# Handing the maximum tiles to the groups of an attention unit by work instead of by count

## The reference, cut to what matters

```python
# 8 sequences of 1024 tokens, width 512, 16 heads of 32
Q, K, V = x @ W_Q.T, x @ W_K.T, x @ W_V.T        # split into 16 heads
attn = einsum('bhqd,bhkd->bhqk', Q, K) * 32 ** -0.5
attn = where(causal, attn, -inf)
y = softmax(attn) @ V
x = layernorm(x + y @ W_O.T)
x = layernorm(x + top1_expert_ffn(x))            # 8 experts, softmax router
```

## Time and profile before

| | |
|---|---|
| time, median of 3 runs | 2583.17 us (2582.08 to 2583.94) |
| profiled execution, its own time | 2585.2 us |
| its span | 2583.5 us |
| PE busy | 2358.2 us, 91% |
| DVE busy | 1452.3 us, 56% |
| ACT busy | 1021.9 us, 40% |
| POOL busy | 870.5 us, 34% |
| mean granted TensorE clock | 0.975 of full speed |

### The profile page before, as it was taken

One profiled execution on the slowest core, in us unless ns is written; L12 is line 12 of the kernel. 1 busy time (PEld: TensorE's weight loads), 2 busy tenths in 40 slices (PEclk: granted clock), 3 DMA queues, 4 the chain that ended last, 5 costly groups with the idle time before them and its releaser, 6 DMA issues. The chain is left out here.

```text
span 2583.5 us, 42271 instructions
## 1 busy us (share of the span) xinstructions
PE 2358.2 (91%) x14336; PEld 1529.8 (59%) x14337; DVE 1452.3 (56%) x3931; ACT 1021.9 (40%) x2089; POOL 870.5 (34%) x1531
## 2 busy tenths in 40 slices
PE   2999999999999999999999999999999999709998
PEld 1754675557554765476546755575547654508886
DVE  2666456735664466536664567355744665346665
ACT  2245414551445234622454245514452345133333
POOL 2223232333223332333232323332233222235665
PEclk9999999999999999999999999999999999859999
DMA  8532153314431353225321533144313421164444
GB/s 298 163 76 82 57 169 85 108 58 123 131 99 66 98 146 85 91 68 170 76 82 57 164 92 105 59 130 124 99 68 106 123 67 42 42 211 133 147 150 120
DMA packets 130937, 282.10 MB, mean 109 GB/s; under 512 B 33026, under 2 KB 42242, under 8 KB 128452
## 3 DMA queue, kind: packets, MB, share of 16 engines
q1 hardware_dynamic: 100920, 208.62, 27.3%
q0 software_dynamic: 28304, 70.64, 9.1%
q10 hardware_dynamic: 1536, 0.53, 0.1%
HBM read 133.04 MB, written 47.53 MB: 70 GB/s over the span
## 5 line engine op out<-in xcount | busy, mean ns | idle before, releaser
L675 ACT ACTIVATE probs<-score 128x512 f32<-128x512 f32 (+3 forms) x1216 | 563.0, 494 | 534.7 <-PE score L991 518.9
L924 PE MATMUL proj<-xt,w_qk 128*128 128x512 f32 x1536 | 428.7, 401 | 60.5 <-DMA w_qk<-w_qk_parts 58.4
L551 POOL TENSOR_SCALAR_AFFINE_SELECT probs<-probs 128x256 f32<-128x256 f32 x512 | 215.6, 423 | 785.3 <-ACT probs L675 782.4
L733 DVE CUSTOM_DVE_ANT_0 maxp<-maxp,mask_qk 128x384 f32<-128x384 f32 (+3 forms) x696 | 323.1, 507 | 233.4 <-PE maxp L979 231.8
L991 PE MATMUL score<-q_stack,k_stack 97*128 97x512 f32 (+2 forms) x1216 | 426.0, 373 | 22.2 <-ACT probs L675 19.8
L979 PE MATMUL maxp<-k_stack,q_stack 96*128 96x512 f32 (+2 forms) x1024 | 330.4, 366 | 35.4 <-DVE tile_max L728 16.3
L924 PEld LDWEIGHTS proj<-xt,w_qk 128*128 128x128 f32 x1536 | 285.6, 191 | 124.0 <-DMA w_qk<-w_qk_parts 49.6
L1011 PE MATMUL y_ps<-probs,v 128*32 128x512 f32 (+3 forms) x3072 | 329.4, 500 | 12.4 <-DVE rows L758 12.2
L1011 PE MATMUL den_ps<-probs,ones_f 128*32 128x512 f32 (+3 forms) x3072 | 320.9, 488 | 0.0
L991 PEld LDWEIGHTS score<-q_stack,k_stack 97*128 97x128 f32 x1216 | 224.6, 189 | 139.2 <-ACT probs L675 90.9
L979 PEld LDWEIGHTS maxp<-k_stack,q_stack 96*128 96x128 f32 x1024 | 181.4, 189 | 165.8 <-DVE tile_max L733 68.2
(11 more groups left out here) (144 smaller groups left out, 2864.7 us busy)
## 6 DMA issues: line engine op xcount, KB each, us to landing
w_qk<-w_qk_parts SPq DMA_DIRECT2D x64, 512.0 KB, 3.8
q_stack<-w_vo_parts SPq DMA_DIRECT2D x16, 2048.0 KB, 8.1
q_stack<-parts SPq DMA_DIRECT2D x512, 64.0 KB, 2.2
k_stack<-parts SPq DMA_DIRECT2D x512, 64.0 KB, 2.2
got<-dispatched SPq DMA_DIRECT2D x75, 257.0 KB, 2.5
xt_raw<-x_t SPq DMA_DIRECT2D x32, 512.0 KB, 4.3
q_stack<-parts POOLq DMA_DIRECT2D x256, 64.0 KB, 2.3
k_stack<-parts POOLq DMA_DIRECT2D x256, 64.0 KB, 2.5
```

The lines of the kernel that those rows point to most:

```text
L551: nc.gpsimd.affine_select(out=block, in_=block, compare_op=ALU.is_ge, fill=0.0, base=0, pattern=[[0, 2], [1, P]], channel_multiplier=-1)\
L675: nc.scalar.activation(probs[:, 4 * (n % PROBS) + h, c:BANK], score_bank(u, 4 * j + h)[:, c:BANK], ACT.Exp, scale=SCALE).then_inc(exp_done ...
L733: top = nc.vector.tensor_tensor_reduce(out=tile, in0=tile, in1=mask_qk[:, BANK - cols:BANK], scale=1.0, scalar=-3.0e38, op0=ALU.add, op1=A ...
L924: mm = nc.tensor.matmul(proj[bank][:, :], w_qk[:, o, ws, k, :], xt[:, xs, k, t * BANK:(t + 1) * BANK], start=c == 0, stop=c == 3 * KT - 1)
```

## The change

The tiles of a unit are no longer dealt out evenly by number over the groups. Each tile gets a work figure (4 for an unmasked tile, and for a diagonal one the sum over its heads of 1 + 3 * columns // 512, which is 4 or 3), each group a room: 2 for groups 6 and 7, and in units 1 and 2 also for groups 2 and 3, else 4. Tiles go in their order to the groups in proportion to room. In unit 0 the tiles now begin at group 1 instead of 2. Both engines read the same function `maxima`, PE at L1078 and DVE at L819.

```diff
-        MAX_GROUPS = (2, 10), (0, 9)
+        MAX_GROUPS = (1, 10), (0, 9)
 ...
             begin, end = MAX_GROUPS[u > 0]
             if not begin <= j < end or u + 1 == UNITS:
                 return []
-            return list(range(MTILES * (j - begin) // (end - begin), MTILES * (j + 1 - begin) // (end - begin)))
+            room = [2 if g in (HALF0 + LAG, HALF0 + LAG + 1) or u and g in (LAG, LAG + 1) else 4 for g in range(end)]
+            work = [4 if diag is None else sum(1 + 3 * cols // BANK for _ in heads) for _, heads, _, cols, diag in MAX_TILES]
+            upto = lambda g: sum(room[begin:g]) * sum(work) / sum(room[begin:end])
+            return [i for i in range(MTILES) if upto(j) <= sum(work[:i]) + work[i] / 2 < upto(j + 1)]
```

## The result

The changed kernel takes 2669.2 us (median of 4 runs, 2666.7 to 2673.6) against 2583.6 us (2582.1 to 2588.1) for the kernel before: ratio 1.033 [1.031, 1.035]. I had predicted 2622 us (2602 to 2639). The sign and the main mechanism were right; the size was less than half of it: +39 us predicted, +85.6 measured. The profiled execution's span is 2665.3 us, 81.8 more than before, and its mean granted clock 0.959 against 0.975. As shares of the span at half clock (twice what is missing from 1) that is about 219 us against 130.

The account below looks back on a forecast made before the run. The prediction took PE's ordered stream as the bound, busy 2358.2 of 2583.5 us. Its terms, -13.6 - 3.3 + 33 + 16.4 + 6.5 = +39 us on a median of 2583.2, gave 2622 us, range 2602 to 2639.

Parts of the forecast that it names:

- Unit 1, group 3, the main term: Unit 1, group 3: DVE takes tile 15 before `divide` and `low`, so PE stands 2.94 us a batch, 23.5 us in all.
- The copies: DVE's copies come later for PE's weighings: +0.7 and +0.5 us a batch in unit 1, +0.45 and +0.55 in unit 2.
- Unit 1's order and distribution: Unit 1: the stand in group 3 and the later copies together, +4.1 us a batch, +33 us.
- Unit 2: Unit 2: later copies and a wait at tile 19, +2.05 us a batch, +16.4 us, bounds 0.5 and 3 a batch.
- at tile 19, +1.05: Unit 2: tile 19 needs tile 16, which waits on DVE behind tile 15 and `divide`: +1.05 us a batch.
- Clock again: Unit 1: the 2.94-us stand loses the clock in four of eight batches, 1.6 us each: +6.5 us.
- Rival 3: Clock falls behind each stand of a batch, also those of 1.4 us in unit 2: 2635 us, chance 0.15.
- The term of unit 0: Unit 0: fewer waits of PE, -1.7 us a batch, -13.6 us, and clock no longer lost, -3.3 us.
- The stalls at tiles 19 and 28: Unit 0: PE's waits of 0.55 us in group 6 and 1.43 us in group 8 were to go.
- less waiting for ACT in group 1: Unit 0, group 1: ten matmuls fill PE's wait for ACT, 0.8 us a batch, of which 0.6 is given back.
- Rival 4: No gain in unit 0: bank waits in group 1 and the copy of group 6 take it; 2636 us, chance 0.10.
- the spacing of DVE's operations: On DVE the next operation starts 0.65 us after a 0.73-us masked reduction; whole lengths would add 3 us in all.

Follow-up runs that it names:

- experiment 1: Changed kernel, but in group 3 of units 1 to 3 DVE takes tile 15 behind the division and the `low`; ratio 1.009 to the kernel before.
- experiment 5: Kernel before, old distribution, but in group 3 of units 1 to 3 DVE takes all four tiles, 15 included, ahead of `divide` and `low`; ratio 1.022.
- experiment 3: Changed kernel, with the first matmul of tile 16 repeated 12 times in unit 1 and 7 times in unit 2; ratio 1.0231 to the kernel before.
- experiment 4: Changed kernel, with POOL's subtraction in unit 2's group 4 held until that group's exps are done; ratio 1.0266 to the kernel before.
- experiment 2: Kernel before, with the new distribution of tiles in unit 0 alone, units 1 and 2 keeping the old one; ratio 0.997 to the kernel before.
- experiment 8: Changed kernel with tile 15 behind division and `low`, and the last two tiles ahead of each copy reduced after copy and transposition; ratio 0.9944 to the kernel before.
- experiment 9: Kernel before, with three tiles ahead of the `low` in unit 0's groups 5 and 7, and one tile held back behind each copy; ratio 0.9906, 2556.6 us.
- experiment 7: Kernel before, but in groups 5 and 7 of unit 0 DVE takes three tiles before the `low`, not two; ratio 0.9966 to the kernel before.
- experiment 6: Changed kernel, with the `low` moved ahead of `divide` in group 3 of units 1 to 3; ratio 1.0244 to the kernel before.

## Why the prediction was right in sign and too small in size

**Right.** *Unit 1, group 3, the main term.* 2.73 us against 2.94, each link of the chain within 0.2 us, and experiments 1 and 5 give and take it. *The copies.* The two in unit 1 rose from 0.26 to 0.96 and by 0.5 us, as reckoned (+0.7, +0.5). Unit 1's order and distribution made 4.6 us a batch for 4.1 predicted. Unit 2's made 2.37 for 2.05, which is partly luck: at tile 19, +1.05 was reckoned, and in the last batch PE waits 0.44 us there; the copies came to +0.65 and, by experiment 1, +0.43 for 0.45 and 0.55 reckoned, and some 0.8 us had no term in the sum.

**The step that failed first: "Clock again", +6.5 us.** It took four losses of 1.6 us, all in unit 1. Measured were thirteen: six in unit 1 (12.8 us, since the stretch was 6.8 us long in three batches) and seven in unit 2 (17.3 us). The rule of the Trainium skill that stood beside that step ("TensorE: Matmul & The Clock Gate", What's actually happening: half clock is the default, activity lifts it) pointed the right way, and experiment 3 bears it out: where PE has matmuls to do through the stand, the clock stays at 1.00 in all eight batches of unit 1. Rival 3, which followed it, was the better forecast, and even that counted half a batch's worth for unit 2.

**The step that failed second: "Unit 2".** Its sum of +2.05 took DVE's operations at their usual durations. Moving tile 15 ahead of `divide` moved the multiply from 1.30 us before the start of POOL's subtraction to 1.10 us behind it, and it took 1.81 us. I listed what is queued behind each moved DVE instruction, and never what runs beside it on POOL. Its own cost is 8.1 us; what it brought on, the 1.56-us wait and so the clock, is most of the 17.3 (experiment 4). The Trainium skill ("SBUF — State Buffer", SBUF: two separate sides) says that a VectorE operation with two SBUF inputs and a GpSimd operation that reads SBUF exclude each other for a whole instruction, and that the one that starts first has it. The trace agrees: the multiply, which reads `rows` and `sums`, started second and grew. The first of POOL's two operations took 2.36 us, about as long as all of them in the kernel before (2.37 to 2.40), and the multiply ended 0.55 us after it. The second of POOL's began beside the multiply and took 2.80 us, 0.44 more.

**The term of unit 0 was twice too large.** -16.9 with its clock was predicted, -8.2 came (-8 in experiment 2). The stalls at tiles 19 and 28 went as reckoned, but PE's waits for ACT grew by 5.1 us in experiment 2, where only unit 0 is changed (in the changed kernel by 7.0, of which 1.9 lie in group 9 of unit 1); the term had counted on less waiting for ACT in group 1 and on none more elsewhere. Group 1 took 1.4 us more, group 5 only 0.8 less. Rival 4 (no gain) was half right.

Together: 48.1 + 44.4 - 8.2 - 2.5 = +81.8 us of span, against +39. Of the difference of 43 us, 17.3 + 6.3 lie in the clock (12.8 less the 6.5 priced), 8.1 in the multiply, 8.7 in unit 0, some 6.5 in the orders of units 1 and 2. The remainder of 4 is the rest of the span and the one spell of half clock that the kernel before had in unit 1.

**A misread source.** For the spacing of DVE's operations the prediction gave half of what the Trainium skill says ("VectorE: DVE Perf Modes", The DRAIN you can't avoid): the section adds that an operation that is not held starts earlier. So the 0.65 us of the earlier trace rows do not contradict it, and the sum, which went by the spacings, is not touched.

**Open.** Why half clock lasted 10.2 us in unit 2 of the changed kernel, 6.8 in experiment 5, and 3.4 or 6.8 in unit 1 was not settled, nor why two stretches had no wait longer than 0.82 us ahead of them (unit 0 of the changed kernel's last batch, unit 2 in one batch of experiment 3). Nor was it tried whether other room figures than 2 and 4 do better once the order is fitted; experiments 8 and 9 only compare this distribution with the even one.

## What to carry to other kernels

In an engine's strict order, look at what is due at the end of the producer's step: it must not stand before work for which another engine already waits. Put the order right before moving amounts; here one slice index in unit 0 (experiment 7) was worth as much as the redistribution of that unit (experiment 2), and another cost three quarters of the loss (experiment 1). Price a new stand of PE with the clock it may lose, and for every instruction that moves in time look at what it newly runs beside on another engine; here 0.69 us became 1.81.

## What the runs showed of the hardware

- Batches in which a stretch of half clock began at a given wait of PE in units 0 to 2 (one traced execution of each kernel), from 1.2 us before its end to 2.5 us after: 0.96 us 0 of 40 (changed, experiments 1, 3, 4, 6); 1.09 us 0 of 8 (experiment 6); 1.31 us 4 of 40 (two in experiment 1, one each in 4 and 6, none in the changed kernel and in 3); 1.43 us 5 of 16 (two before, three in experiment 5); 1.56 us 13 of 14 (changed, experiment 6, both with a 1.31-us wait two groups ahead); 1.72 us 7 of 7 (experiment 5); 2.73 us 13 of 16 (changed, experiment 4); 2.78 us 8 of 8 (experiment 5). These were waits for DVE; waits of 1.0 to 1.1 us for the copy in unit 2's group 6 had it 0 of 27 times, waits of 1.0 to 1.5 us for a DMA 3 of 15. The stretches were 3.4, 6.8 or 10.2 us long, and each cost 1.0 to 3.3 us.
- A `tensor_tensor` of 128x512 float32 on DVE with both inputs in SBUF took 0.69 us alone and 1.81 us when it began 1.10 us after POOL's `tensor_tensor`; the PSUM reductions next to it kept their 0.68 us. POOL's operation that began beside the multiply took 2.80 us, the one before it 2.36.
- Repeating matmuls that nobody needs, in time that PE would have stood, made the kernel some 25 us faster (experiment 3).
